# Layer norm sums as four products per two tiles, an earlier evacuation and moved copies in a fused convolution and scan kernel

## What is computed

```python
xs  = groupnorm(x) @ in_proj_w.T                  # 768 -> 1536 channels
xs  = silu(depthwise_conv3x3(xs) + conv_b)        # u
x_dbl = xs @ x_proj_w.T                           # 48 + 4 + 4 columns
dt, Bs, Cs = split(x_dbl)
delta = softplus(dt @ dt_w.T + dt_b)
dA  = exp(delta * A);  dBu = delta * u * Bs       # 4 states per channel
states = scan(a2 * a1, a2 * x1 + x2)              # along the 4096 tokens
y   = sum(states * Cs) + D * u
y   = (y - mean(y)) * rsqrt(var(y) + 1e-5) * ln_g + ln_b   # over the 1536 channels
x   = x + y @ out_proj_w.T                        # 1536 -> 768
```

## Time and profile before

| what | value |
|---|---|
| runs | 4144.58, 4155.73, 4157.65 us; median 4155.73 |
| profiled execution, own time | 4160.17 us |
| its span | 4158.4 us |
| mean granted TensorE clock | 0.93 of full speed |
| TensorE busy | 3677.8 us (88%) |
| VectorE busy | 2941.7 us (71%) |
| ScalarE busy | 2308.3 us (56%) |
| GpSimd busy | 2240.8 us (54%) |
| layer 0's loop | from about 100 to 3000 us |

### The profile page before, as it was taken

The page is one execution under the profiler, slowest core; times in us unless marked ns, Lnnn a source line. Parts: engine busy times, 40 slices in busy tenths (PEclk is TensorE's granted clock), DMA queues, the critical chain, the costliest instruction groups (busy, mean ns, idle before and its releaser), DMA issues. The chain is left out here.

```text
span 4158.4 us, 37515 instructions
## 1 busy us (share of the span) xinstructions
PE 3677.8 (88%) x10728; PEld 1784.8 (43%) x10728; DVE 2941.7 (71%) x4066; ACT 2308.3 (56%) x3726; POOL 2240.8 (54%) x1361
## 2 busy tenths in 40 slices
PE   5866798999998999999998999987869989999899
PEld 4422233333333343333333333332338638886287
DVE  4579989889898788888989889897523363333632
ACT  1356667766766666766767667665324441244511
POOL 0258878788888777877878778888400000000000
PEclk7888899999999999999999999988889979999699
DMA  6243454455554445445554455545443203511023
GB/s 255 98 131 100 104 148 124 131 139 132 134 129 131 128 113 147 123 131 133 127 142 123 130 133 127 144 96 130 106 165 107 80 31 122 180 64 61 31 91 122
DMA packets 192531, 502.92 MB, mean 121 GB/s; under 512 B 17916, under 2 KB 29756, under 8 KB 187336
## 3 DMA queue, kind: packets, MB, share of 16 engines
q1 hardware_dynamic: 164680, 399.86, 29.2%
q0 software_dynamic: 27648, 100.68, 13.2%
HBM read 335.06 MB, written 64.75 MB: 96 GB/s over the span
## 5 line engine op out<-in xcount | busy, mean ns | idle before, releaser
L543 PE MATMUL p_op<-uy,wout_ring 128*128 128x512 f32 x2304 | 1117.2, 634 | 95.7 <-DVE x_res L851 95.7
L527 PE MATMUL p_in<-xn,win_ring 128*128 128x512 f32 (+1 forms) x2304 | 1067.2, 614 | 145.8 <-ACT halo L660 110.5
L811 DVE TENSOR_TENSOR_SCAN p_da<-p_da,state,g_ring 128x512 f32<-128x512 f32 x672 | 827.2, 1277 | 157.0 <-ACT p_da L623 143.8
L783 POOL TENSOR_TENSOR g_ring<-du,B_bc 128x2048 f32<-128x2048 f32 x192 | 870.1, 4532 | 15.3 <-DMA B_bc<-bc_scratch 0.4
L837 DVE SCALAR_TENSOR_TENSOR p_cv<-v_slots,conv_w,p_cv 128x512 f32<-128x512 f32 x960 | 721.6, 752 | 175.0 <-ACT p_cv L682 156.8
L543 PEld LDWEIGHTS p_op<-uy,wout_ring 128*128 128x128 f32 x2304 | 443.6, 201 | 780.0 <-issue 633.8
L527 PEld LDWEIGHTS p_in<-xn,win_ring 128*128 128x128 f32 x2304 | 447.1, 198 | 739.0 <-issue 738.8
L623 ACT ACTIVATE p_da<-delta,A 128x512 f32<-128x512 f32 x768 | 498.2, 681 | 396.3 <-DVE g_ring L821 392.1
L821 DVE TENSOR_TENSOR g_ring<-p_da,C_bc 128x1024 f32<-128x1024 f32 x384 | 470.2, 1224 | 24.0 <-DMA C_bc<-bc_scratch 23.1
L1067 PE MATMUL banks<-x_split,w_split 128*128 128x512 f32 x1152 | 450.9, 391 | 13.4 <-issue 7.1
L1068 PE MATMUL banks<-x_split,w_split 128*128 128x512 f32 x1152 | 450.2, 391 | 0.0
(11 more groups left out here) (169 smaller groups left out, 4209.7 us busy)
## 6 DMA issues: line engine op xcount, KB each, us to landing
g_ring<-g_ring POOLq DMA_DIRECT2D x192, 512.0 KB, 4.9
win_ring<-in_win SPq DMA_DIRECT2D x192, 384.0 KB, 3.1
wout_ring<-wout_scratch SPq DMA_DIRECT2D x192, 384.0 KB, 3.5
xc<-x_scratch SPq DMA_DIRECT2D x32, 1536.0 KB, 7.0
x_res<-in_x SPq DMA_DIRECT2D x96, 256.0 KB, 3.5
x_scratch<-x_res SPq DMA_DIRECT2D x96, 256.0 KB, 4.6
out<-xc SPq DMA_DIRECT2D x16, 1536.0 KB, 5.8
xn<-in_x SPq DMA_DIRECT2D x12, 1536.0 KB, 6.9
```

The lines of the kernel that those rows point to most:

```text
L527: last = nc.tensor.matmul(p_in[:, 0:n], WR[:, i % NW, t, :], XN[:, t, off:off + n], start=(t == 0), stop=(t == XT - 1))
L543: last = nc.tensor.matmul(p_op[:], OR[:, e % NO, k - h * HALF, :], ucol(c * K + k), start=(k == 0), stop=(k == K - 1))
L783: nc.gpsimd.tensor_tensor(G[:, i % NG], DU[:].unsqueeze(1).broadcast_to([P, NS, N]), BB[:, c % 2], ALU.mult).then_inc(s_dbu, 1)
L811: nc.vector.tensor_tensor_scan(bank, bank, G[:, i % NG, n, :], init, ALU.mult, ALU.add)\
```

## The change

- The norm sums of two tiles are taken together, in even slots only: four 32-column products (L569, L570, each for h = 0 and 1) write the four quarters of p_ln's partitions. SQ has two halves. The sums are copied with all 128 partitions, and the two products with pick have 64 rows each instead of 32.
- evacuate stands behind the decays of L_SCAN (and ahead of silu) in all slots but the group slots; in group slots it stands between the second and the third softplus. Slot 0 is unchanged.
- The first x_dbl copy moves from the end of slot 2 behind the centre tap and the square of slot 3; the second from there behind the two decays of slot 3. The fold product stands one product later in in_proj.
- B_bc has one buffer instead of two; its load waits until all B products of the chunk before are done.

```diff
-        SQ = sb("sq", [P, N])
+        SQ = sb("sq", [P, 2, N])
-        p_sq, p_y = p_ln[0:32, :], p_ln[32:64, :]
+        p_sq, p_y = (p_ln[0:32, :], p_ln[32:64, :]), (p_ln[64:96, :], p_ln[96:P, :])
...
-                        wait(sp, s_dbu, K * (c - 1))
-                        sp.dma_start(BB[:, c % 2].rearrange("p n t -> p (n t)"),
+                        wait(sp, s_dbu, K * c)
+                        sp.dma_start(BB[:].rearrange("p n t -> p (n t)"),
...
-                        if t == 2 and fold_of is not None:
+                        if t == 3 and fold_of is not None:
                             fold_xproj(fold_of)
...
                     i = tile(S, L_SQ)
-                    if i is not None:
+                    if i is not None and i % 2:
                         c, j = divmod(i, K)
-                        if j == 0:
+                        if j == 1:
                             wait(pe, s_ls, c)
                         pe.wait_ge(s_y, i + 1)
                         pe.wait_ge(s_sq, i + 1)
-                        nc.tensor.matmul(p_y, ones32[:], ucol(i), start=(j == 0), stop=(j == K - 1))
-                        nc.tensor.matmul(p_sq, ones32[:], SQ[:], start=(j == 0), stop=(j == K - 1))\
-                          .then_inc(s_ln, 1)
+                        for h in range(2):
+                            nc.tensor.matmul(p_y[h], ones32[:], ucol(i - 1 + h), start=(j == 1), stop=(j == K - 1))
+                            nc.tensor.matmul(p_sq[h], ones32[:], SQ[:, h], start=(j == 1), stop=(j == K - 1))\
+                              .then_inc(s_ln, 1)
...
-                        nc.tensor.matmul(p_dt[:, 0, :], pick[32:64, :], LS[32:64, :], start=True, stop=True)\
+                        nc.tensor.matmul(p_dt[:, 0, :], pick[64:P, :], LS[64:P, :], start=True, stop=True)\
...
-                        wait(act, s_ln, i)
-                        nc.scalar.activation(SQ[:], ucol(i), ACT.Square).then_inc(s_sq, 1)
+                        wait(act, s_ln, 2 * (i // 2))
+                        nc.scalar.activation(SQ[:, i % 2], ucol(i), ACT.Square).then_inc(s_sq, 1)
                     c = chunk_at(S, S_XP[2] + 1)
                     if c is not None:
-                        act.wait_ge(s_xf, c + 1)
-                        nc.scalar.activation(XD[:], p_dt[:, 1, :], ACT.Copy).then_inc(s_xd, 1)
+                        act.wait_ge(s_xp, 2 * (c + 1))
+                        wait(act, s_bw, 16 * c)
+                        nc.scalar.activation(XD[:], p_dt[:, 0, :], ACT.Copy).then_inc(s_xe, 1)
...
                     if i is not None:
                         decay(i, 2)
                         decay(i, 3)
+                    c = chunk_at(S, S_XP[2] + 1)
+                    if c is not None:
+                        act.wait_ge(s_xf, c + 1)
+                        nc.scalar.activation(XD[:], p_dt[:, 1, :], ACT.Copy).then_inc(s_xd, 1)
...
-                    if new is not None and S % K and not grouped:
+                    q = group_at(S)
+                    if new is not None and S % K and q is None:
                         evacuate(new)
...
-                        for i in range(NSP * q, NSP * (q + 1)):
-                            softplus(i)
+                        softplus(NSP * q)
+                        softplus(NSP * q + 1)
+                        if new is not None:
+                            evacuate(new)
+                        softplus(NSP * q + 2)
+                        softplus(NSP * q + 3)
...
-                    if new is not None and S % K and grouped:
-                        evacuate(new)
...
-                    c = chunk_at(S, S_XP[2])
-                    if c is not None:
-                        act.wait_ge(s_xp, 2 * (c + 1))
-                        wait(act, s_bw, 16 * c)
-                        nc.scalar.activation(XD[:], p_dt[:, 0, :], ACT.Copy).then_inc(s_xe, 1)
```

More of the change, by code:

```diff
@@ L169, in layer0 @@
         bm = sb("b_m", [P, XT])
-        pick = sb("pick", [64, P])
+        pick = sb("pick", [P, P])
         fold = sb("fold", [P, P])
@@ L292, in layer0 @@
         UY = sb("uy", [P, NU, N])
-        BB = sb("B_bc", [P, 2, NS, N])
+        BB = sb("B_bc", [P, NS, N])
         CB = sb("C_bc", [P, NS, N])
@@ L319, in layer0 @@
         s_wor = [sem(f"s_wor{n}") for n in range(NO)]
-        s_xin, s_bw, s_b, s_c = sem("s_xin"), sem("s_bw"), [sem("s_b0"), sem("s_b1")], sem("s_c")
+        s_xin, s_bw, s_b, s_c = sem("s_xin"), sem("s_bw"), sem("s_b"), sem("s_c")
         s_gv, s_gp, s_ga, s_st = sem("s_gv1"), sem("s_gp1"), sem("s_ga1"), sem("s_st1")
@@ L476, in _ @@
                         sp.wait_ge(s_bw, 16 * (c + 1))
-                        wait(sp, s_dbu, K * (c - 1))
-                        sp.dma_start(BB[:, c % 2].rearrange("p n t -> p (n t)"),
+                        wait(sp, s_dbu, K * c)
+                        sp.dma_start(BB[:].rearrange("p n t -> p (n t)"),
                                      bc_d[c, 0:NS].rearrange("n t -> (n t)").partition_broadcast(P))\
-                          .then_inc(s_b[c % 2], 16)
+                          .then_inc(s_b, 16)
                     c = chunk_at(S, 16)
@@ L581, in _ @@
                         pe.wait_ge(s_delta, deltas_by(S))
-                        nc.tensor.matmul(p_dt[:, 0, :], pick[32:64, :], LS[32:64, :], start=True, stop=True)\
+                        nc.tensor.matmul(p_dt[:, 0, :], pick[64:P, :], LS[64:P, :], start=True, stop=True)\
                           .then_inc(s_mean, 1)
-                        nc.tensor.matmul(p_dt[:, 1, :], pick[0:32, :], LS[0:32, :], start=True, stop=True)\
+                        nc.tensor.matmul(p_dt[:, 1, :], pick[0:64, :], LS[0:64, :], start=True, stop=True)\
                           .then_inc(s_e2, 1)
@@ L670, in _ @@
                     new = tile(S, 0)
-                    grouped = S % 4 > 1
                     if new is not None and S % K and (new // K) % CPB == 0:
@@ L729, in _ @@
                         act.wait_ge(s_ln, K * (c + 1))
-                        nc.scalar.activation(LS[0:64, :], p_ln[0:64, :], ACT.Copy).then_inc(s_ls, 1)
+                        nc.scalar.activation(LS[:], p_ln[:], ACT.Copy).then_inc(s_ls, 1)
                     i = tile(S, L_CH)
@@ L781, in _ @@
                         wait(pool, s_y, i - NG + 1)
-                        pool.wait_ge(s_b[c % 2], 16 * (c // 2 + 1))
+                        pool.wait_ge(s_b, 16 * (c + 1))
                         nc.gpsimd.tensor_tensor(G[:, i % NG], DU[:].unsqueeze(1).broadcast_to([P, NS, N]),
-                                                BB[:, c % 2], ALU.mult).then_inc(s_dbu, 1)
+                                                BB[:], ALU.mult).then_inc(s_dbu, 1)
                     if y is not None:
```

## The result

| | before | changed |
|---|---|---|
| median of the runs | 4153.9 us | 4127.8 us |
| range | 4144.6 to 4157.7 | 4123.5 to 4137.1 |
| profiled execution, own time | 4160.2 us | 4137.1 us |
| its span | 4158.4 us | 4135.3 us |
| mean granted TensorE clock | 0.930 | 0.922 |

The median before includes one execution more than the table ahead of the prediction had. The ratio is 0.9943 with an interval from 0.9918 to 0.9969: 26 us faster, where 50 were forecast. The direction is right and the time lies in the forecast's range, but the gain is half of what was forecast.

The account below looks back on a forecast made before the run. No single engine bounds it: a loop runs through VectorE, TensorE and ScalarE. 2.8 us a chunk gave 39 in fourteen, with 5, 2 and 4 elsewhere 50 us: 4110, or 4106 in the median's terms; range 4080 to 4130.

Parts of the forecast that it names:

- Group slots, norm products: Slots 3, 7, 11: without norm products in odd slots, out_proj starts earlier; slot 7 gains 0.9 us, four products take 0.99.
- The first rival: Even slots: the fourth norm product runs alone, 0.4 us gained per chunk, 4142 us; chance 0.15.
- Chunk boundary: Slots 0 to 3: TensorE's chain decides, with earlier square, faster layer norm and out_proj, fewer norm products; 3.4 us gained.
- x_dbl's copies at nothing: Slots 2 and 3: TensorE decides, and the second copy is ready 1.1 us before in_proj ends; it costs nothing.
- One B buffer at nothing: B's load after GpSimd's last product with the old B: 9 us remain to land, so no cost.
- Slots 8 to 0: Slots 10 and 11: missing norm product gains 0.99, early evacuation costs VectorE 1.8; second pair only 0.1 us earlier.
- Slots 4 to 8: Slots 4 to 6: 5 us residual-add wait, slow out_proj in slot 5, late in_proj; VectorE loses 1.6 us in slot 7.
- The sum: Per chunk 0.9 + 0.1 + 3.4 - 1.6 = 2.8 us of 172.6; fourteen chunks give 39 us.
- The 11 us outside the regular chunks: Gains booked beyond the fourteen chunks: 5 us in chunk 8, 2 in the first chunk, 4 in the tail.
- Slot 5 at the full clock: Rival: slots 5 and 0 stay at full clock, 2.6 us more per chunk, 4070 us; chance 0.15.
- The slower one: Rival, slots 5 and 9: all 12 out_proj passes at half speed, 10.8 us, total 4179; chance 0.13.
- 0.9 + 1.6 us a chunk: Early evacuation: slot 11's 0.99 gain shrinks to 0.1, and VectorE loses 1.6 in slot 7 behind slot 5's slow out_proj.

Follow-up runs that it names:

- serial version: The changed kernel with the evacuation behind silu, and the norm products of a pair one behind the other instead of four at once: 4115.4 us.
- the filler run: The changed kernel with products of zeros added between in_proj and out_proj of slots 5 and 9: 4098.1 us.

## Why the prediction was half right

**Group slots, norm products: right.** The four products side by side take 1.00 us, and half of out_proj in slot 7 is bound by the residual add (1843.95). The first rival, the fourth product by itself, didn't come. VectorE's idleness ahead of slot 8 fell by 0.7 us, where 0.9 was forecast.

**Chunk boundary: right in size, with some luck.** The forecast was 3.4 us between the scans of slots 0 and 4, and 61.5 - 57.9 = 3.6 was measured as a mean, but only 2.7 (61.0 to 58.2) in the chunk from which it was worked out. The new 3.70 us of VectorE's idleness do lie beside TensorE's chain: with the evacuation behind silu they are gone and the stretch stays 57.9. x_dbl's copies at nothing: shown by the run with them alone. The moved copy itself waits 2.7 us in all 16 chunks together, where it waited 6.21 in one. One B buffer at nothing: GpSimd waits for B at two of the 16 loads, 2.8 us in all, and the norm sums alone had the one buffer and gained 51 us.

**Slots 8 to 0, a step that failed.** The forecast had a gain of 0.1 us; measured is a loss of 57.4 - 56.8 = 0.6. VectorE's 1.8 us in slot 11 were right (1.66 as a mean), and so was the length of the stretch in the changed kernel, 1851.25 to 1908.86 us, 57.6. What was wrong is what it was compared with. In the reference chunk out_proj of slot 9 took 8.24 us and the stretch 57.7. But the kernel before has two kinds of chunks. In five of the ten averaged ones this out_proj took 6.95 to 7.11 us, in one of them after the same 4.21 us of waiting:

```profile
2055.55 7.11 PE L543 MATMUL p_op<-uy,wout_ring 128*128 128x512 f32 x12 [4.21 <-DVE x_res L851]
```

In these five the stretch took 56.1 to 56.3 us, and in the other five, with 7.96 to 8.48, 57.1 to 57.7. In the changed kernel all ten are of the long kind, 8.13 to 8.41. As means that is 7.6 against 8.3 us, about what the forecast missed here. So the prediction had slot 9's slow out_proj equally long in both kernels, a term of nothing, where it was some 0.6 us a chunk. Why the changed kernel has only long ones stays open.

**Slots 4 to 8, a second step that failed by as much.** The mechanism came as forecast, 4.56 us of waiting, a slow out_proj of 8.12, ScalarE's wait of 2.06, VectorE's of 2.07. The forecast was 1.6 us lost, of which slot 7 gives back 0.9, so 0.7 net; measured is 55.0 - 53.5 = 1.5. VectorE loses 1.9 us ahead of slot 7 instead of 1.6 and gets 0.7 back ahead of slot 8 instead of 0.9, which is 0.5 of the missing 0.8. Here too the reference chunk was a long one in the kernel before: 54.2 us against 55.3, only 1.2 lost.

**The sum.** The forecast was 2.8 us a chunk and 171.9 - 170.3 = 1.6 was measured, which in 14 chunks is 22 us instead of 39. The 11 us outside the regular chunks are missing altogether: the profiled executions differ by 23.1 us in all, and by 17.6 in layer 0. At the start the first scan comes 5.2 us later (273.8 instead of 268.7, and 283.5 with the early evacuation alone), and the first stretch from slot 4 to 8 takes 49.4 us instead of 53.9, so that next to nothing is left of the loss, but nothing of the 2 us of gain either. At the end, over the last twelve tiles, where in_proj is done, the changed kernel takes 130.8 us instead of 128.8, where 4 were booked as a gain. The 2 us at the start stood in the prediction without a working.

**The rivals.** Slot 5 at the full clock: no, it was slow in every regular chunk. The slower one, 10.8 us for an out_proj all at half speed: no, it took 7.6 to 8.4 in the regular chunks. But its direction was right: slot 9's out_proj did get longer as a mean, and ScalarE's wait ahead of silu carried that to VectorE. The larger lesson lies in a question that wasn't put: the text named the early evacuation in slots 2, 6 and 10 as a cost and booked it at 0.9 + 1.6 us a chunk, but never summed the change without it. That sum alone was a reason to expect a better kernel, and it is: 4076. There the part's cost is 1.9 + 1.5 us a chunk. So the 1.6 was nearly right, and the 0.9 was half of what it cost.

## What to carry to other kernels

Price every part against the schedule that the other parts leave: the early evacuation cost nothing in the old kernel, since another engine was later at the same meeting point, and 52 us once that one was sped up. A copy that waits for an engine belongs behind the work that doesn't wait, above all behind table loads and decays that the slowest engine needs. Compare a changed stretch with the mean of that stretch over many chunks, since one chunk's slow TensorE stretch was worth more than the effect. And when two single executions are compared, read the times at the end of the part that was changed: here the part that nobody touched differed by up to 20 us.

## What the runs showed of the hardware

How long TensorE stays slow after a wait doesn't follow from the wait's length. After the same 5.97 us of waiting in slot 9, out_proj took 8.2 to 8.4 us in every ordinary chunk of the changed kernel and 6.9 to 7.2 in those of the kernel with the evacuation behind silu; in the latter's serial version it took 8.0 to 8.4 after only 5.12. The kernel before had 6.95 and 7.96 after the same 3.86. At the full clock these 12 passes take 5.42. Nor does the wait's length alone tell whether a stretch is slow: in the filler run the clock was 0.68 after 1.83 us, where others had come before, and the changed kernel had 5.42 us after 1.95.

Products of zeros with 32 columns hold the full clock as well as real work does (1.00 in the window behind them, in slot 9 of the ten averaged chunks; in slot 5 two chunks still had 7.12 us after waits of 2.03 and 2.18). And four 32-column float32 products with four different inputs stream at once at no cost over two: 1.00 us against 0.99.
